# Attention of a macaron block on eight cores: q and k of four heads made with tokens on partitions and turned by DMA transposes

## The chip, the cores and the metric

One Trainium2 chip; the program runs on eight of its NeuronCores, one sequence of the batch on each, and the cores exchange nothing. The metric is the device time of the slowest core in microseconds. TensorE does the matmuls (PE in the profile), VectorE (DVE), ScalarE (ACT) and GpSimd (POOL) the rest, and SyncE (SP) issues DMAs. DMAs are issued from SP and from POOL; those of POOL also convert the f32 weights to bf16.

## The reference

The input x is 8 x 2048 x 1024. Three layers follow one another; this is the core of them:

```python
x = x + 0.5 * ffn(layernorm(x))          # r = sigmoid(xr W_r), k = relu(xk W_k)^2, r * (k W_v)
# attention, 16 heads, dh = 64, rank r = 48
x = layernorm(hidden, ln1_g, ln1_b)
Q = einsum('bsd,dhr,hre->bhse', x, q_U, q_V) + q_b
K = einsum('bhsr,hrd->bhsd', einsum('bsd,dhr->bhsr', x, k_U), k_V) + k_b
V = einsum('bhsr,hrd->bhsd', einsum('bsd,dhr->bhsr', x, v_U), v_V) + v_b
scores = einsum('bhse,bhte->bhst', Q, K) / 8, causal; attn = softmax(scores)
attn_out = ctx @ out_U @ out_V + out_b;  h = hidden + attn_out
h + (gelu(layernorm(h) @ fc1_U @ fc1_V + fc1_b) @ fc2_U @ fc2_V + fc2_b)
x = x + 0.5 * ffn(layernorm(x))          # the same weights again
```

## The kernel before

The kernel has four stages on each core: phase 0 (the first ffn), phase 1 (attention), phase 2 (output projection and MLP), phase 3 (the second ffn). Every engine runs a program of its own, in order; semaphores tie them together. Tokens are worked in four blocks of 512. The normalised input of attention lies in x1T, features on partitions, 8 chunks of 512 tokens for each block.

Scores are computed in the rank space: the q weight is Wq = q_U (q_V k_V^T), 49 wide with a column for the k bias, so that a head's score is the product of a 49-row q and a 49-row k. Two heads are a pair (p, 0 to 7); they lie at partitions 0 and 64. Before the change a unit Q or K makes q or k of one pair for one block: for each chunk c, two matmuls with 64 weight columns each and 512 tokens moving. It comes out with features on partitions, VectorE adds the bias on eviction from PSUM and writes Qr or Kr (two buffers of each), and scores read them there. A unit V makes v of eight heads for 128 tokens with tokens as weights and 384 columns of vU moving.

All this is laid out by a planner. Attention of a pair is 20 steps; a step g is two tiles of 128 keys by 512 queries of both heads. In a step TensorE does the scores of two tiles (pe_qk), then the pieces of other units that slots[g] lists, then the context of the step before (pe_av). ScalarE turns each tile into exponentials (act_exp), two PSUM tiles SD taking turns; VectorE multiplies the diagonal tiles by a mask, evicts units (dve_unit) in the order of their last matmul, and normalises. Within a pair, step 20p + j(j+1) + n belongs to query block j; its last two steps are on the diagonal and have fewer columns. fill() gives each step g a budget scale(g) * room(g), with room 4 for a full step, 3.5 and 2 for the diagonal ones; matmuls(u) and weight(u) are the chunks of a unit and the price of one; each job has a first step and a due step. Units use two PSUM banks UB in turn, so a unit starts when the unit before its neighbour is evicted (u_ev). The units early run in the last block of phase 0, prelude ahead of step 0. Other units: G and Wq build the q weight, A, ob, bo, W fold the output weights, fb folds a bias, after which VectorE scales f1U.

SP issues in phase 0 the transposes of x1T and the spills of X to DRAM (sp_tr, sp_spill), in phase 1 the packs of the normalised context into CN (sp_pack: four or five small copies for each pair and block). POOL issues the weight loads in an order written out by hand (pool_pair_weights, pool_phase1), tied to the count of scores (pool_at). In the last pair it reloads the spilled rows into S.

## Time and profile before

| what | value |
|---|---|
| median of 3 runs | 1071.65 us (1070.51 to 1195.31) |
| the profiled execution | 1070.4 us |
| its span, slowest of 8 cores | 1068.6 us (1064.0 to 1068.6) |
| TensorE busy in the span | 1016.2 us (95%) |
| VectorE, ScalarE, GpSimd busy | 549.5, 537.0, 187.5 us |
| granted clock of TensorE, eight cores | 0.992 to 0.995 |
| matmul instructions | 6278 |

The time is device time; the span goes from the first to the last instruction of one core, and the two differ by 1.8 us in the profiled execution. A granted clock of 1.0 is TensorE's upper level (2.4 GHz), 0.5 the lower (1.2 GHz). The busy time of an engine counts overlapping instructions once.

### The profile page before, as it was taken

To read this page: it belongs to the slowest core of one execution; us is meant where nothing else is said; L and a number is where in the kernel's file an instruction comes from. 1 tells how busy PE (TensorE), PEld (TensorE's weight loads), DVE (VectorE), ACT (ScalarE), POOL (GpSimd) and SP (SyncE) were. 2 spreads that over 40 slices of the span, in tenths; PEclk is the share of its full clock that TensorE was granted. 3 is DMA by queue.
4 is the path that set the end of the run, shared out by engine and by line. 5 is a ranking of instruction groups with operands and counts; after the bars stand their busy time and mean duration, and the time that the engine had idled before them with its cause. 6 is when DMAs were issued, how large, how long until landed. Compare 5 with 4: busy or idle time off the path is not lost.

```text
span 1068.6 us, 16930 instructions; the slowest of 8 cores (1064.0 to 1068.6 us)
## 1 busy us (share of the span) xinstructions
PE 1016.2 (95%) x6278; PEld 459.5 (43%) x6278; DVE 549.5 (51%) x1013; ACT 537.0 (50%) x646; POOL 187.5 (18%) x185
## 2 busy tenths in 40 slices
PE   3999999999999999898998999999999999999998
PEld 1444444454444444344343444444444444444443
DVE  6568979654646546566368980012120433734523
ACT  2335354267777787876775454333333354341321
POOL 2021423400000001110022137670000000023030
PEclk9999999999999999999999999999999999999999
DMA  9982377642110116750087899952300026041212
GB/s 167 209 220 69 90 142 164 121 100 69 31 27 17 28 28 98 110 81 9 8 207 213 112 123 154 211 96 48 63 16 1 1 40 115 5 119 79 40 79 79
DMA packets 94686, 95.89 MB, mean 90 GB/s; under 512 B 67856, under 2 KB 75152, under 8 KB 93328
## 3 DMA queue, kind: packets, MB, share of 16 engines
q0 software_dynamic: 20112, 52.74, 27.4%
q1 hardware_dynamic: 74496, 42.07, 17.0%
q8 instruction: 54, 0.88, 0.3%
q14 instruction: 24, 0.20, 0.1%
HBM read 91.94 MB, written 16.78 MB: 102 GB/s over the span
## 4 chain that ended last, share of the span: by engine, by line
PE 74%; DVE 14%; issue 5%; ACT 4%; DMA 2%; SPq 1%; DVEq 0%; ACTq 0%
PE ub L905 11%; PE db L1414 10%; PE db L1380 10%; PE db L355 7%; PE db L369 7%; PE sd L1040 7%; PE db L381 6%; PE ct L1075 5%; PE ub L915 3%; DVE st L420 3%; PE db L1393 3%; ACT AT L1050 2%; PE db L1367 2%; PE db L1352 2%; PE ub L957 2%
## 5 line engine op out<-in xcount | busy, mean ns | idle before, releaser
L1050 ACT ACTIVATE AT<-sd 128x1024 bf16<-128x1024 f32 (+1 forms) x320 | 267.7, 897 | 83.2 <-PE sd L1040 82.8
L1463 ACT ACTIVATE HM<-db,csts 128x512 bf16<-128x512 f32 x128 | 80.8, 683 | 138.9 <-PE db L1380 138.9
L1414 PE MATMUL db<-HM,f2U 128*128 128x512 bf16 x512 | 120.3, 379 | 1.3 <-ACT HM L1463 1.3
L1380 PE MATMUL db<-P,f1V 128*128 128x512 bf16 x512 | 120.3, 379 | 1.0 <-ACT P L1451 1.0
L1040 PE MATMUL sd<-Qr,Kr 64*128 64x512 bf16 (+3 forms) x640 | 96.1, 352 | 9.3 <-ACT AT L1050 8.6
L1075 PE MATMUL ct<-AT,VA 128*64 128x512 bf16 (+3 forms) x640 | 87.1, 351 | 3.5 <-DVE AT L1057 3.5
L1414 PEld LDWEIGHTS db<-HM,f2U 128*128 128x128 bf16 x512 | 49.9, 98 | 62.1 <-issue 2.9
L1380 PEld LDWEIGHTS db<-P,f1V 128*128 128x128 bf16 x512 | 50.0, 98 | 61.7 <-issue 1.7
L1557 DVE CAST P<-db 128x1024 bf16<-128x1024 f32 x4 | 4.9, 1224 | 137.9 <-PE db L1414 137.9
L905 PE MATMUL ub<-x1T,Wq 128*64 128x512 bf16 x512 | 69.3, 389 | 1.8 <-DVE tta L409 1.6
L905 PE MATMUL ub<-x1T,kU 128*64 128x512 bf16 x512 | 67.2, 383 | 0.1
L355 PE MATMUL db<-XKa,wk 128*128 128x512 bf16 x256 | 57.6, 387 | 5.6 <-DVE XKa L470 5.6
L414 POOL TENSOR_TENSOR X<-X,tta 128x1024 f32<-128x1024 f32 x16 | 43.5, 2736 | 105.9 <-DVE XKa L470 90.6
L1040 PEld LDWEIGHTS sd<-Qr,Kr 64*128 64x128 bf16 x640 | 28.5, 93 | 77.0 <-issue 71.6
L369 PE MATMUL db<-wr,XRa 128*128 128x512 bf16 x256 | 58.1, 387 | 0.6 <-DVE XRa L484 0.6
L381 PE MATMUL db<-wv,KAa 128*128 128x512 bf16 x256 | 56.0, 379 | 1.4 <-DMA wv<-wvT 1.4
L355 PE MATMUL db<-XKb,wk 128*128 128x512 bf16 x256 | 56.1, 379 | 0.0
L369 PE MATMUL db<-wr,XRb 128*128 128x512 bf16 x256 | 55.9, 379 | 0.0
L390 ACT ACTIVATE krla<-db 128x1024 bf16<-128x1024 f32 x16 | 16.4, 1023 | 74.4 <-PE db L355 52.4
L381 PE MATMUL db<-wv,KAb 128*128 128x512 bf16 x240 | 52.6, 379 | 0.1
L915 PE MATMUL ub<-vU,x1T 128*64 128x384 bf16 x512 | 48.5, 329 | 2.0 <-DVE VA L991 1.1
L1075 PEld LDWEIGHTS ct<-AT,VA 128*64 128x64 bf16 x640 | 35.4, 110 | 33.1 <-issue 8.6
(161 smaller groups left out, 1335.4 us busy)
## 6 DMA issues: line engine op xcount, KB each, us to landing
S<-xs POOLq DMA_DIRECT2D x32, 512.0 KB, 10.1
xs<-X SPq DMA_DIRECT2D x4, 2048.0 KB, 9.2
x_out<-S SPq DMA_DIRECT2D x15, 512.0 KB, 2.6
wr<-wrT POOLq DMA_DIRECT2D x4, 1024.0 KB, 18.8
X<-x_in SPq DMA_DIRECT2D x2, 2048.0 KB, 13.9
f1V<-fc1V POOLq DMA_DIRECT2D x16, 256.0 KB, 4.4
f2U<-fc2U POOLq DMA_DIRECT2D x32, 128.0 KB, 6.3
CN<-cs SPq DMA_DIRECT2D x112, 24.0 KB
```

Source lines behind the costliest of these rows:

```text
L355: m = pe.matmul(DB[p][:, TB * h:TB * (h + 1)], f.wk(c, dk), f.XK[:, TB * c:TB * (c + 1)], start=c == 0, stop=c == CH - 1)
L369: m = pe.matmul(DB[2 * t % 4][:, TB * h:TB * (h + 1)], XR[:, TB * c + 128 * t:TB * c + 128 * (t + 1)], f.wr(c)[:, TB * h:TB * (h + 1)], st ...
L381: m = pe.matmul(DB[2 * t % 4 + 1][:, TB * h:TB * (h + 1)], f.KA[:, TB * c + 128 * t:TB * c + 128 * (t + 1)], f.wv(c)[:, TB * h:TB * (h + 1 ...
L414: pool.tensor_tensor(xt, xt, f.tt[(4 * b + t) % len(f.tt)][:, :], ALU.add)._wait_ge(F.kv, 4 * b + t + 1).then_inc(F.add, 1)
L905: m = pe.matmul(bank[o:o + 64, :], w[:, 128 * c + o:128 * c + o + 64], x1T[j][:, TB * c:TB * (c + 1)], start=c == 0, stop=c == CH - 1)
L915: m = pe.matmul(bank[o:o + 64, 0:384], x1T[t // 4][:, x0:x0 + 64], vU[:, w0 + 384 * c:w0 + 384 * (c + 1)], start=c == 0, stop=c == CH - 1)
L1040: m = pe.matmul(SD[q % 2][:, TB * s + off:TB * (s + 1)], Kr[p % 2][64 * s:64 * s + 64, 128 * i:128 * (i + 1)], Qr[p % 2][64 * s:64 * s + 6 ...
L1050: act.activation(c3(AT[q % 4])[:, :, off:TB], c3(SD[q % 2])[:, :, off:TB], AF.Exp, scale=0.125)._wait_ge(a_qk, q + 1).then_inc(a_exp, 1)
L1075: m = pe.matmul(CT[k % 2][64 * s:64 * s + 64, off:TB], VA[p // 4][:, 512 * i + 64 * h:512 * i + 64 * (h + 1)], AT[q % 4][:, TB * s + off:T ...
L1380: m = pe.matmul(bank[:, TB * e:TB * (e + 1)], f1V[ic // 8][:, 1024 * pc + 128 * (ic % 8):1024 * pc + 128 * (ic % 8 + 1)], P1[b][:, TB * pc ...
L1414: m = pe.matmul(DB[2 + p2 // 2][:, TB * (p2 % 2):TB * (p2 % 2 + 1)], f2U[ic // 8][:, 512 * (ic % 8) + 128 * p2:512 * (ic % 8) + 128 * (p2 ...
L1463: m = act.activation(HM[i % 4][:, TB * e:TB * (e + 1)], DB[job_db[("H", b, i)]][:, TB * e:TB * (e + 1)], AF.Gelu_apprx_tanh, bias=scol("fc ...
```

## The change

Q and K units are replaced by QK units. A group G is four heads (pairs 2G and 2G+1). QK(G, t) makes q and k of the four heads for 128 tokens: the tokens of x1T are the weights (two halves of 64), and the 8 x 49 = 392 columns of WQK (GC) move, q and k weights of the pairs side by side. VectorE adds qbB, a row of biases repeated on all partitions, and writes the result into a quarter of ST, each 49 columns padded to 64; ST's padding is cleared once, at the end of phase 0. Then SP issues two DMA transposes of 128 x 256 (sp_qk), one for each pair, into one of three pair buffers QS (q in the first 2048 columns, k in the second). Scores of an even pair wait for the transposes (d_qt) at each query block; a VectorE eviction waits until the transposes four units earlier have landed. The weights of a group come by pool_group_weights: one load of WQK with zero columns in the q places, which the evictions of Wq then fill, and two of qUT. Four Wq and a qb are made for each group. The planner gets new prices, due steps and scales: 1.12 up to step 130 and 0.85 from 131 to 156; V of the upper heads may start at step 12, A at step 92, and W is spread over steps 131 to 156. Some buffers move to other places, and the loads of vVT, outV, fc1_V and the last group's weights take other points in POOL's order. sp_phase1 interleaves the transposes with the packs.

The core of the diff:

```diff
+GC = 8 * (RQ + 1)
...
-    kUp = np.zeros((128, NP, CH, 128), np.float32)
+    kUp = np.zeros((128, NP // 2, CH, 2, 2, 2, RQ + 1), np.float32)
     for h in range(NH):
         s, p = h % 2, h // 2
-        kUp[:, p, :, 64 * s:64 * s + RQ] = kU[:, h, :].reshape(CH, 128, RQ).transpose(1, 0, 2)
+        kUp[:, p // 2, :, p % 2, 1, s, :RQ] = kU[:, h, :].reshape(CH, 128, RQ).transpose(1, 0, 2)
...
-    Qr = [at("Qr%d" % i, T, BF16, 24 + 8 * i) for i in range(2)]
-    Kr = [at("Kr%d" % i, T, BF16, 28 + 8 * i) for i in range(2)]
+    QS = [at("QS%d" % i, 2 * T, BF16, (24, 32, 176)[i]) for i in range(3)]
     CN = [at("CN%d" % b, 6 * TB, BF16, (40, 48, 56, 160)[b]) for b in range(NB)]
     cs = [at("cs%d" % b, TB, BF16, (46, 54, 62, 166)[b]) for b in range(NB)]
     vU = at("vU", 2 * CH * 384, BF16, 72)
-    Wq = [at("Wq%d" % i, 1024, BF16, 84 + 2 * i) for i in range(2)]
+    ST = at("ST", 4 * 512, BF16, 84)
+    WQK = at("WQK", CH * GC, BF16, 120)
+    qbB = at("qbB", GC, F32, 126.125)
     VA = [at("VA%d" % i, NT * 512, BF16, 88 + 16 * i) for i in range(2)]
-    qUT = [at("qUT%d" % i, D, BF16, 120 + 2 * i) for i in range(2)]
-    kU = [at("kU%d" % i, 1024, BF16, 124 + 2 * i) for i in range(2)]
+    qUT = [at("qUT%d" % i, D, BF16, (142, 140)[i]) for i in range(2)]
     qVT, kVTb = at("qVT", 1024, BF16, 136), at("kVTb", 1024, BF16, 138)
-    Gs, vVT = at("Gs", 1024, BF16, 140), at("vVT", 1024, BF16, 142)
+    qbr = at("qbr", 1024, BF16, 136)
+    Gs, vVT = at("Gs", 1024, BF16, 128), at("vVT", 1024, BF16, 130)
...
+        for t in range(4):
+            sp_qk(sp, 0, t)
...
+        dve.memset(ST[:, :], 0.0).then_inc(q_z, 1)
+        dve.memset(qbB[:, :], 0.0).then_inc(q_z, 1)
+        dve.memset(qbB[:, :].rearrange("p (i k s e) -> p i k s e", i=2, k=2, s=2)[:, :, 1, :, RQ:RQ + 1],
+                   1.0)._wait_ge(q_z, 2).then_inc(q_z, 1)
...
+            if i == 1:
+                dve.wait_ge(d_bconst, 16)
+                dve.tensor_copy(qbr[:, :].rearrange("p (q e) -> p q e", e=128),
+                                bsl("qb", 0, NP).unsqueeze(2).to_broadcast([128, NP, 128])).then_inc(q_z, 1)
...
-    early = [("G", 0), ("G", 1), ("qb",), ("Wq", 0, 0), ("Wq", 0, 1)]
-    prelude = [("Q", 0, 0), ("K", 0, 0)] + [("V", 0, t) for t in range(4)]
+    early = [("G", 0), ("G", 1), ("Wq", 0, 0), ("Wq", 0, 1), ("Wq", 1, 0), ("Wq", 1, 1), ("qb", 0)]
+    prelude = [("QK", 0, t) for t in range(4)] + [("V", 0, t) for t in range(4)]
...
-        return [("Q", 0, j), ("K", 0, j)] + [("V", 0, t) for t in range(4 * j, 4 * j + 4)]
+        return [(kind, 0, t) for kind in ("QK", "V") for t in range(4 * j, 4 * j + 4)]
     def matmuls(u):
-        return {"Q": CH, "K": CH, "V": CH, "W": 6}.get(u[0], 1)
+        return {"QK": CH, "V": CH, "W": 6}.get(u[0], 1)
...
-        return {"V": 0.75, "Wq": 1.5, "A": 1.5, "ob": 6, "bo": 6, "fb": 12}.get(u[0], 1)
+        return {"QK": 0.77, "V": 0.75, "Wq": 1.0, "qb": 0.5, "A": 1.5, "ob": 6, "bo": 6, "fb": 12}.get(u[0], 1)
...
-    def pair_jobs(p):
-        due = [step_of(p, j, 0) - 2 for j in range(NB)]
-        jobs = [(STEPS * (p - 1) - 2, STEPS * (p - 1) + 1 if p > 1 else due[0], ("Wq", p, h))
-                for h in range(2)]
-        for kind in "QK":
-            jobs += [(STEPS * (p - 1), due[j], (kind, p, j)) for j in range(NB)]
+    def group_jobs(G):
+        g = STEPS * (2 * G - 1)
+        jobs = [(g - 4, g + 1, ("Wq", p, h)) for p in (2 * G, 2 * G + 1) for h in range(2)]
+        jobs += [(g - 4, g + 1, ("qb", G))]
+        jobs += [(g, step_of(2 * G, t // 4, 0) - 3, ("QK", G, t)) for t in range(NT)]
         return jobs
-    fill([(0, 1, u) for u in block_units(1)], 0, 1, lambda g: 8.0)
-    fill([(2, 5, u) for u in block_units(2)], 2, 5, lambda g: 3.2)
-    fill([(6, 11, u) for u in block_units(3)], 6, 11, lambda g: 2.1)
-    jobs = [j for p in range(1, NP) for j in pair_jobs(p)]
-    jobs += [(STEPS, step_of(4, t // 4, 0) - 2, ("V", 1, t)) for t in range(NT)]
-    merge = [("A", jc, h) for jc in range(6) for h in range(2)] + [("ob",), ("bo", 0), ("bo", 1), ("fb",)]
-    jobs += [(STEPS * 5 + 4, STEPS * 7 - 1, u) for i, u in enumerate(merge)]
-    fill(jobs, 11, STEPS * 7 - 1, lambda g: 1.5 if g < 88 else 1.35)
-    fill([(STEPS * 7, STEPS * 7 + 13, ("W", hc, h)) for hc in range(6) for h in range(2)],
-         STEPS * 7, STEPS * 7 + 13, lambda g: 1.6)
+    fill([(0, 1, u) for u in block_units(1)], 0, 1, lambda g: 9.0)
+    fill([(2, 5, u) for u in block_units(2)], 2, 5, lambda g: 3.7)
+    fill([(6, 11, u) for u in block_units(3)], 6, 11, lambda g: 2.35)
+    jobs = [j for G in range(1, NP // 2) for j in group_jobs(G)]
+    jobs += [(12, step_of(4, t // 4, 0) - 2, ("V", 1, t)) for t in range(NT)]
+    merge = [("A", jc, h) for jc in range(6) for h in range(2)] + [("ob",)]
+    jobs += [(STEPS * 4 + 12, STEPS * 6 - 1, u) for u in merge]
+    jobs += [(STEPS * 6 + 4, STEPS * 7 - 1, u) for u in (("bo", 0), ("bo", 1), ("fb",))]
+    jobs += [(STEPS * 6 + 11, STEPS * 8 - 4, ("W", hc, h)) for hc in range(6) for h in range(2)]
+    fill(jobs, 12, STEPS * NP - 4, lambda g: 1.12 if g < STEPS * 6 + 11 else 0.85)
...
-        elif kind in ("Q", "K"):
-            p, j = u[1], u[2]
-            if p == 0 and i0 == 0:
-                pe.wait_ge(b_aff, j + 1)
-            if kind == "K":
-                if j == 0 and i0 == 0:
-                    pe.wait_ge(d_ku[p % 2], 16 * (p // 2 + 1))
-                w = kU[p % 2]
-            else:
-                if j == 0 and i0 == 0:
-                    pe.wait_ge(u_ev, done("Wq", p, 1))
-                w = Wq[p % 2]
+        elif kind == "QK":
+            G, t = u[1], u[2]
+            if i0 == 0:
+                if t == 0:
+                    pe.wait_ge(u_ev, done("Wq", 2 * G + 1, 1))
+                if G == 0 and t % 4 == 0:
+                    pe.wait_ge(b_aff, t // 4 + 1)
             for c in range(i0, i1):
                 for o in (0, 64):
-                    m = pe.matmul(bank[o:o + 64, :], w[:, 128 * c + o:128 * c + o + 64],
-                                  x1T[j][:, TB * c:TB * (c + 1)], start=c == 0, stop=c == CH - 1)
+                    x0 = TB * c + 128 * (t % 4) + o
+                    m = pe.matmul(bank[o:o + 64, 0:GC], x1T[t // 4][:, x0:x0 + 64],
+                                  WQK[:, GC * c:GC * (c + 1)], start=c == 0, stop=c == CH - 1)
...
+            if u[1] == 0:
+                pe.wait_ge(q_z, 4)
+            for i in range(2):
+                p = 2 * u[1] + i
+                m = pe.matmul(bank[:, 128 * i:128 * (i + 1)], qbr[:, 128 * p:128 * (p + 1)],
+                              kVTb[:, 128 * p:128 * (p + 1)], start=True, stop=True)
         elif kind == "Wq":
             p = u[1]
...
-            m = dve.tensor_copy(qbias[:, :], bank[:, 0:NP])
+            if u[1] == 0:
+                dve.wait_ge(q_z, 3)
+            m = dve.tensor_copy(
+                qbB[:, :].rearrange("p (i k s e) -> p i k s e", i=2, k=2, s=2)[:, :, 0, :, :],
+                bank[:, 0:256].rearrange("p (i s e) -> p i s e", i=2, s=2)[:, :, :, 0:RQ + 1])
...
+            p, h = u[1], u[2]
+            if p % 2 == 0 and h == 0:
+                dve.wait_ge(d_ku, 16 * (p // 2 + 1))
+            dst = WQK[:, GC * 4 * h:GC * 4 * (h + 1)].rearrange("p (c e) -> p c e", e=GC)
+            o = 4 * (RQ + 1) * (p % 2)
+            m = dve.tensor_copy(
+                dst[:, :, o:o + 2 * (RQ + 1)].rearrange("p c (s e) -> p c s e", s=2),
+                bank[:, :].rearrange("p (c s e) -> p c s e", c=4, s=2)[:, :, :, 0:RQ + 1])
+        elif kind == "QK":
+            G, t = u[1], u[2]
+            n = NT * G + t
+            if t == 0:
+                dve.wait_ge(u_ev, done("qb", G))
+            if n >= 4:
+                dve.wait_ge(d_qt[t % 4], 32 * (n // 4))
+            else:
+                dve.wait_ge(q_z, 3)
+            dst = ST[:, 512 * (t % 4):512 * (t % 4 + 1)].rearrange("p (h e) -> p h e", e=64)
+            m = dve.tensor_tensor(dst[:, :, 0:RQ + 1],
+                                  bank[:, 0:GC].rearrange("p (h e) -> p h e", e=RQ + 1),
+                                  qbB[:, :].rearrange("p (h e) -> p h e", e=RQ + 1), ALU.add)
...
-            pe.wait_ge(u_ev, max(done("Q", p, j), done("K", p, j)))
+        if i == 0 and p % 2 == 0:
+            for k in range(4):
...
+                pe.wait_ge(d_qt[k], 32 * (2 * p + j + 1))
...
+                          QS[p % 3][64 * s:64 * s + 64, T + 128 * i:T + 128 * (i + 1)],
+                          QS[p % 3][64 * s:64 * s + 64, TB * j + off:TB * (j + 1)],
...
+    def sp_qk(sp, G, t):
+        if t == 0 and G == 0:
+            for b in (1, 2):
+                sp.wait_ge(d_sp[b], 16)
+                sp.wait_ge(F0.z, 4 * group("B", b) + 4)
+        if t == 0 and G == 1:
+            sp.wait_ge(F0.add, 16)
+        if t == 0 and G:
+            sp.wait_ge(a_qk, 40 * (2 * G - 1))
+        sp.wait_ge(u_ev, done("QK", G, t))
+        for i in range(2):
+            sp.dma_start_transpose(c3(QS[(2 * G + i) % 3], T)[:, :, 128 * t:128 * (t + 1)],
+                                   ST[:, 512 * (t % 4) + 256 * i:512 * (t % 4) + 256 * (i + 1)]).then_inc(
+                                       d_qt[t % 4], 16)
     def sp_phase1(sp):
+        for p, j, n in steps():
+            g = step_of(p, j, n)
+            for u, i0, i1 in slots[g]:
+                if u[0] == "QK" and i1 == matmuls(u):
+                    sp_qk(sp, u[1], u[2])
+            for k in range(32):
+                if last_step[k] + NORM == g:
+                    sp_pack(sp, k)
         for k in range(32):
-            sp_pack(sp, k)
+            if last_step[k] + NORM >= STEPS * NP:
...
+    def pool_group_weights(pool, G):
+        if G:
+            pool.wait_ge(u_pe, done("QK", G - 1, NT - 1))
+        pool.dma_start(WQK[:, :], dram["kU"][:, CH * GC * G:CH * GC * (G + 1)]).then_inc(d_ku, 16)
+        for p in (2 * G, 2 * G + 1):
+            pool.dma_start(qUT[p % 2][:, :], dram["qUT"][:, D * p:D * (p + 1)]).then_inc(d_qu[p % 2], 16)
...
+                    pool_group_weights(pool, 0)
...
+        pool_group_weights(pool, 1)
+        pool.dma_start(bo_bc[:, :], dram["outb_row"].partition_broadcast(128)).then_inc(d_bc, 16)
+        pool.dma_start(fb_bc[:, :], dram["fc2b_row"].partition_broadcast(128)).then_inc(d_bc, 16)
+        pool_group_weights(pool, 2)
...
+            if jc == 3:
+                pool_group_weights(pool, 3)
...
+        for q in (1, 0):
             for i in range(4):
-                pool_at(pool, 5, 8 + 3 * (4 * q + i))
+                pool_at(pool, 6 - q, 8 + 6 * i)
...
+            pool.wait_ge(u_pe, max(done("QK", 3, NT - 1), done("ob")))
+            for k in range(4):
+                pool.wait_ge(d_qt[k], 32 * NT)
```

## Rows read from the trace of the kernel before

**Rows 1.** Windows, attention: length, busy (count) of five engines, clock, DMA share, GB/s.
```profile
216.00:574.00 358.00, 340.33 (x3104) 152.79 (x3100) 198.96 (x409) 274.55 (x326) 31.05 (x59) 0.99 0.34 68
```

**Rows 2.** Windows, pairs 1, 4 and 5, first exponential to first exponential.
```profile
273.87:317.68 43.81, 42.99 (x384) 18.92 (x382) 23.42 (x47) 33.65 (x40) 2.13 (x4) 1.00 0.20 34
...
404.09:443.81 39.72, 36.79 (x310) 15.31 (x308) 20.30 (x43) 33.23 (x40) 9.52 (x18) 1.00 0.81 118
443.81:489.06 45.25, 41.54 (x406) 18.96 (x404) 27.67 (x56) 33.61 (x40) 4.24 (x8) 1.00 0.44 67
```

**Rows 3.** Timeline of PE, two steps of pair 1: start, us, engine, line.
```profile
305.50 0.61 PE L1040 MATMUL sd<-Qr,Kr 64*128 64x512 bf16 x4
306.04 1.49 PE L905 MATMUL ub<-x1T,kU 128*64 128x512 bf16 x12
307.36 0.60 PE L1075 MATMUL ct<-AT,VA 128*64 128x512 bf16 x4
307.89 0.60 PE L1040 MATMUL sd<-Qr,Kr 64*128 64x512 bf16 x4
...
308.88 1.14 PE L915 MATMUL ub<-vU,x1T 128*64 128x384 bf16 x12
```

**Rows 4.** Timeline of PE, steps with no unit, at the end of pair 4.
```profile
436.88 0.39 PE L1040 MATMUL sd<-Qr,Kr 64*128 64x512 bf16 x2 [0.52 <-ACT AT L1050]
...
438.71 0.39 PE L1040 MATMUL sd<-Qr,Kr 64*128 64x512 bf16 x2 [0.52 <-ACT AT L1050]
```

**Rows 5.** Timeline of PE, prelude and step 0.
```profile
213.09 2.79 PE L915 MATMUL ub<-vU,x1T 128*64 128x384 bf16 x32 [0.51 <-DVE VA L991]
215.81 0.55 PE L1040 MATMUL sd<-Qr,Kr 64*128 64x512 bf16 x4
216.29 1.92 PE L905 MATMUL ub<-x1T,Wq 128*64 128x512 bf16 x16
```

**Rows 6.** Groups by line, PE: busy, mean ns of one, idle before.
```profile
L905 PE MATMUL ub<-x1T,kU 128*64 128x512 bf16 x512 | 67.2, 383 | 0.1
```

**Rows 7.** Timeline of PE, a lightly filled step of pair 4.
```profile
430.39 0.79 PE L1040 MATMUL sd<-Qr,Kr 64*128 64x512 bf16 x4
...
432.53 0.77 PE L1040 MATMUL sd<-Qr,Kr 64*128 64x512 bf16 x4
```

**Rows 8.** Timeline of PE around A and Wq units, pair 5.
```profile
474.35 0.85 PE L924 MATMUL ub<-vVT,oU 128*128 128x128 bf16 x8 [0.64 <-DVE AoT L995]
...
485.58 0.62 PE L950 MATMUL ub<-oV,oB 128*64 128x512 bf16 x4 [0.86 <-DVE Wq L970]
```

**Rows 9.** Windows, after fb.
```profile
503.00:510.00 7.00, 6.30 (x32) 2.09 (x32) 2.96 (x7) 4.57 (x5) 0.00 (x0) 0.52 0.05 12
```

**Rows 10.** Timeline of PE, last block of phase 0.
```profile
180.94 0.34 PE L879 MATMUL ub<-bcst,kVTb 128*128 128x1 bf16 x8 [1.34 <-DVE Gs L966]
```

**Rows 11.** Timeline of DVE, last block of phase 0.
```profile
181.20 2.66 DVE L550 TENSOR_SCALAR x1T<-x1T,csts 128x512 bf16<-128x512 bf16 x8
...
183.86 0.68 DVE L970 CAST Wq<-ub 128x512 bf16<-128x512 f32 x1
...
190.64 2.70 DVE L550 TENSOR_SCALAR x1T<-x1T,csts 128x512 bf16<-128x512 bf16 x8 [2.47 <-DMA x1T<-zt]
```

**Rows 12.** DMA issues, 208 to 222: KB each, us to landing.
```profile
xs<-X SPq DMA_DIRECT2D x1, 2048.0 KB, 11.0
...
x1T<-zt SPq DMA_TRANSPOSE x4, 4.8
```

**Rows 13.** DMA issues, 182 to 190.
```profile
x1T<-zt SPq DMA_TRANSPOSE x4, 3.2
```

**Rows 14.** DMA issues, 420 to 440.
```profile
kU<-kU POOLq DMA_DIRECT2D x1, 256.0 KB, 8.4
```

**Rows 15.** Timeline of SP, four transposes in a row, phase 3.
```profile
949.20 5.39 SPq L1580 DMA_TRANSPOSE zTb<-zu  x4
```

**Rows 16.** DMA issues, 147 to 170.
```profile
x1T<-zt SPq DMA_TRANSPOSE x4, 13.9
```

82 lines of the change are left out of this document (23 added, 59 removed).

## The prediction, made before the kernel ran

> **What bounds it now.** The cores lie within 0.4% of each other, so one core tells of all. First I read the window of the whole attention stage [rows 1]: TensorE is busy 340.3 of its 358 us, ScalarE 274.6, VectorE 199.0. TensorE's order of work is the path there, and only its busy time or its gaps can give time back. The stage behind (574 on) keeps its code and I leave it as it is. Second, the stretches of single head pairs, each with 40 exponentials [rows 2]: pair 1 takes 43.8 us with TensorE full, pair 4 takes 39.7 with a gap of 2.9, pair 5 takes 45.3 with a gap of 3.7. ScalarE needs some 33.5 us of each. Third, single steps in the timeline, because a step is what the planner fills. A full step with six chunk pairs of projection lasts 2.39 us, scores to scores, and TensorE never waits in it [rows 3]. A full step with no projection lasts 1.83 us, with a wait of 0.52 for the exponential [rows 4]. So filled steps are TensorE's and empty ones ScalarE's.
>
> **Price of a chunk.** A chunk pair is the two half-column matmuls of one chunk. Old Q or K: 8 pairs take 1.92 us [rows 5], 6 take 1.49 [rows 3], so 0.215 each. V is built as the new units are (tokens as weights, 384 columns moving): 16 pairs take 2.79 us [rows 5], 6 take 1.14 [rows 3], so 0.165. The new unit moves 392 columns: 0.168. The number of pairs stays: 256 for K, which is the 512 matmuls of its row [rows 6], and as many for Q; new, 4 groups x 16 x 8 = 512. Saved on TensorE: 512 x 0.047 = 24 us.
>
> **How steps turn that into time.** A full step holds scores (0.53), the fill F, context (0.53) [rows 3]. Between the empty and the crowded step neither engine is full: scores of one step wait for exponentials of the step before, and behind them on TensorE lie fill and context. I take the largest of 1.83, 1.64 + F/2 and 1.07 + F; the middle one is half of two exponentials (1.94) plus TensorE's chain (1.34 + F). The step at 430.39 has F 0.87 and measured 2.14 [rows 7]; the formula gives 2.07. Diagonal steps go alike with floors of 1.73 and 0.87. The planner is arithmetic in the code, so I worked both plans out from it. The old one has F about 1.3 in most full steps and leaves 17 steps empty; the new one has 1.0 in most, 0.65 to 0.87 in the last 25, and leaves 12 empty. By pair the old steps sum to 56.1, 42.9, 42.8, 42.9, 39.1, 41.1, 40.4, 40.0 = 345; measured 358, and the 13 between are lumps, below. The new ones: 59.2, 38.5, 38.8, 38.6, 37.0, 38.6, 38.8, 35.6 = 325. So the steps give 20 us: the 24 of TensorE and 5 of gaps, less 9 that full steps near 2.1 lose in the chain between two engines.
>
> **Lumps.** A unit's bank must be evicted before the next but one unit starts. Old: A units, three or four to a step, wait 0.64 for VectorE's eviction, two Wq 0.86 [rows 8]. The new plan puts four Wq and one qb into steps 16, 56 and 96: three evictions on the path, some 1.8 us a time, 5.4 in all against 3 for the old ones. A units: 2.0 against 3. After fb came f1U's scaling in front of a mask and half the clock for 7 us [rows 9]: 3 us; the scaling now meets no diagonal step: 1.5. First steps and last context stay at 3.3. New 12, old 12.5: nothing.
>
> **End of phase 0.** VectorE gets two clears ahead of G's evictions, for which TensorE already waits 1.34 us [rows 10]. The trace has no clear of this size. ST is 2048 bf16 columns; x1T's scaling does 512 in 0.33 (2.66 for 8) and Wq's cast in 0.68 [rows 11], so 1.4 to 2.7; I take 2.0, as a clear has no bf16 source to profit from, and 0.4 for qbB. On the path 2.4, bounds 1.5 and 3.2. The Trainium skill, page "VectorE: DVE Perf Modes", section "Zero memsets can be issued as uint32 (trn2)", says that a clear takes a cycle per element whatever the type; by it the clear is nearer the upper bound, and the sum half a microsecond longer. Two more Wq and a larger qb: 0.6 on TensorE. qbr's copy and three evictions (some 2.7 us) are hidden by VectorE's wait of 2.47 for x1T [rows 11] and its waits for phase 0's matmuls; without that cover 2 us. Sum +3.
>
> **Start of attention.** The prelude is 32 x (0.168 + 0.165) against 16 x 0.215 + 32 x 0.165: +1.9. Then the first scores wait for eight transposes. SP issues block 3's 2 MB spill just before them; it landed 11.0 us after issue, and the x1T transposes behind it 4.8 after theirs [rows 12], against 3.2 on a quiet queue [rows 13]. Spill at 211, landed by 221, transposes 1 us behind; V covers TensorE until 219.9. Stall 2.0, bounds 0 and 6. The old wait of 0.51 for V's eviction goes [rows 5]. First scores 215.8 + 3 + 1.9 + 2.0 - 0.5 = 222.2, +6.4.
>
> **Elsewhere.** Each later group's first use comes at least seven steps (15 us) behind its last eviction, against 3 to 8 us of landing: nothing; without that cover some 3 us at each of 12 gates. On SP, the packs (4 or 5 issues each) now stand between the transposes, in step order. VectorE's new wait for a quarter of ST has masks and normalisations behind it, and TensorE's context waits for those; four units are 12 us. WQK and qUT of the last group go out at step 91 among outV and f1U, where a 256 KB load took 8.4 us [rows 14]; they are needed at step 96, 11 us on: 0.5. S8's reload waits for the last W, now 7 us before the end of attention instead of 13; the next stage has 21 us before it: nothing, or 2 if it delays x2T.
>
> **Sum.** 1068.6 - 20 + 6.4 + 0.5 = 1055.5 of span. The profiled run took 1.8 more than its span, so 1057.3, and the median is 1.25 above that run: 1058 (-1.3%). Within 2% is about what a measurement of this kernel can't tell from no change.
>
> **Rivals.** (a) The forecast, 1058, with 1051 to 1065: 0.50.
> (b) All is covered: clears at the lower bound, no stall at the start, the Wq steps as cheap as the formula: 1058 - 1 - 2 - 5.4 - 1.5 (fb) = 1048. For it: VectorE is busy little over half of attention. Against: such steps cost in the old trace. 0.18.
> (c) A small transpose costs SP what a large one does: four took 5.39 us to issue [rows 15], 1.35 each. Eight end at 222.3 and land by 225, +3; four of x1T and eight more hold step 2 until 241 instead of 237, +5: 1066. Against: the small ones hold a quarter of the data. The Trainium skill, "DMA: Bandwidth & Descriptors", section "Rules for kernel authors", says that transfers under 64 KB pay mostly overhead and are best joined; these are 64 KB. 0.15.
> (d) The steps don't give it back: freed matmul time becomes waits for exponentials, full steps at 2.2 instead of 2.1. 90 x 0.1: 1067. Against: [rows 7]. 0.10.
> (e) Slower: the ring of four. Behind a spill and loads four transposes took 13.9 us to land [rows 16]. Once landing and eviction exceed four units' pitch, 12.8 us, VectorE stops and its masks with it. At 17.6 a unit costs 4.4 us instead of 3.2: 48 x 1.2 = 58, about 1115. Against: a pair's DMA share of 0.20 [rows 2]. 0.07.
>
> Faster by over 2% (under 1050): (b) and the edge of (a), 0.19. Slower: (e), 0.07. Same: 0.74. The range 1044 to 1072 leaves out (e) and the far ends of (b), (c) and (d).
>
> **What would show it.** QK runs of 16 matmuls in 1.5 us; full steps 2.1 apart; first scores near 222, behind a wait for a DMA; steps 16, 56, 96 over 3.5; G's eviction 2.4 later. It is wrong if TensorE waits for transposes after step 0, or VectorE for ST, or if the clears cost nothing.

## The result: slower by 5.3%, and the profile after

| what | value |
|---|---|
| median of the changed kernel | 1129.01 us (4 runs), before beside it 1071.79 us |
| ratio | 1.0533, 95% interval 1.0509 to 1.0557 |
| predicted | 1058 us, range 1044 to 1072 |
| profiled execution | 1127.43 us, span of its slowest core 1125.8 us |
| spans of the cores | 1115.3 to 1125.8 us, granted clock 0.965 to 0.974 |

In some executions, of the kernel before and of changed ones alike, the cores of one die ran at a lower granted clock and some per cent longer; the ratios leave these out, and so do the times of experiments 3 and 6, where they would move the median by 4 and 7 us.

The kernel is slower, and on all cores. The first view is the window of the attention stage and of what follows it, on core 3: length, then busy time (count) of PE, PEld, DVE, ACT and POOL, the granted clock, the DMA share and GB/s.

```profile
216.00:630.00 414.00, 337.49 (x3122) 160.39 (x3118) 185.43 (x408) 273.51 (x327) 28.14 (x54) 0.93 0.40 77
630.00:1125.00 495.00, 486.81 (x2244) 219.26 (x2244) 189.81 (x315) 177.76 (x237) 104.08 (x91) 1.00 0.41 83
```

Attention grew from 358 us [rows 1] to some 403 (first scores 228.08, last context 630.9; before 215.8 and 573.6), and the stages behind it are as long as they were. TensorE is busy no longer than before, 337.5 against 340.3 us, and that at a granted clock of 0.93 against 0.99, so it has indeed less to do. It stands still for 76 us of the window, where it stood for 18. What it waits for is the next view, the waits of PE and DVE in attention (total us, times, longest):

```profile
PE sd L1066 <- DMA QS<-ST: 43.4, 7, 14.0
PE sd L1066 <- ACT AT L1076: 16.3, 46, 0.5
PE ct L1101 <- DVE AT L1083: 9.3, 7, 3.1
...
DVE ST L1009 <- DMA QS<-ST: 40.3, 15, 4.7
```

Scores (sd) wait seven times for the transposes of q and k. VectorE waits fifteen times for a quarter of ST that a transpose still has to read; behind these waits stand masks, and TensorE waits for masks in its turn (the third row; before, 3.5 us in four waits). These are two of the signs that the prediction gave for being wrong. The chain that ended last, by engine and by line, names a queue:

```profile
PE 50%; SPq 18%; DVE 14%; DMA 8%; issue 6%; ACT 3%; POOL 1%; DVEq 0%; ACTq 0%; POOLq 0%
SPq L1166 12%; PE db L1471 10%; PE db L1437 9%; PE db L384 5%; PE db L358 5%; SPq L1148 5%; PE db L372 4%; DMA X<-x_in 4%; DMA QS<-ST 3%; PE sd L1066 3%; DVE st L423 3%; PE db L1450 2%; PE ct L1101 2%; PE ub L931 2%; PE db L1424 2%
```

L1166 issues the transposes of q and k, L1148 the packs. SP's timeline in pair 1 and the first part of pair 2 shows how (start, length, line, count):

```profile
317.63 4.96 SPq L1166 DMA_TRANSPOSE QS<-ST  x4
322.69 3.65 SPq L1148 DMA_DIRECT2D CN<-cs  x5
326.44 5.56 SPq L1166 DMA_TRANSPOSE QS<-ST  x4
332.10 3.62 SPq L1148 DMA_DIRECT2D CN<-cs  x5
335.82 10.38 SPq L1166 DMA_TRANSPOSE QS<-ST  x8
346.29 3.62 SPq L1148 DMA_DIRECT2D CN<-cs  x5
350.01 14.03 SPq L1166 DMA_TRANSPOSE QS<-ST  x10
```

There is no gap between the rows: the queue is full from 317 to 384 us. A transpose of 128x256 takes 1.2 us to issue, a pack 0.72, so a QK unit (two transposes) and its share of packs cost SP 4.2 us (the 16 units of group 1 in 67 us), where the plan brings a unit every 3.2 us. A second kind of loss is at the ends of the groups, here step 92, the first scores that read the last transposes of group 2, in PE's timeline, and SP's and POOL's issues before it:

```profile
468.35 0.57 PE L1101 MATMUL ct<-AT,VA 128*64 128x512 bf16 x4
482.91 1.04 PE L1066 MATMUL sd<-QS 64*128 64x512 bf16 x4 [13.99 <-DMA QS<-ST]
```
```profile
467.51 3.53 SPq L1166 DMA_TRANSPOSE QS<-ST  x2
```
```profile
467.51 0.53 POOL L1241 DMA_DIRECT2D WQK<-kU  x1 [1.31 <-PE sd L1066]
```

The last two transposes go out in the same instant as the 784 KB weight load of the next group and land 12 to 14 us later; the median of all is 2.4. The same happens at steps 12 (wait 10.55 us) and 52 (4.86). The weight load is not alone there: two 256 KB loads of qUT go with it, at step 92 five loads of outV (256 KB each) too, and at step 12 two broadcast loads of biases (512 KB each). After a long wait the matmuls run at 1.2 GHz for a while: the granted clock is 0.50 from 484 to 490 us.

The sums by pair, in us from first scores to first scores (the last one to the last context); "formula" are the steps as the prediction worked them out:

| pair | 0 | 1 | 2 | 3 | 4 | 5 | 6 | 7 |
|---|---|---|---|---|---|---|---|---|
| before | 57.6 | 43.8 | 43.5 | 43.0 | 39.7 | 45.3 | 43.8 | 41.1 |
| formula | 59.2 | 38.5 | 38.8 | 38.6 | 37.0 | 38.6 | 38.8 | 35.6 |
| changed | 80.9 | 41.0 | 51.8 | 40.6 | 62.7 | 40.9 | 47.1 | 37.9 |

Pairs 1, 3, 5 and 7, which begin with buffers filled long ago, have become shorter than before, as meant, though 2.0 to 2.5 us longer than the formula. Pairs 0, 2, 4 and 6, where a new group begins, carry the loss.

### The profile page after: what moved, and what is told of

It reads as the page before. It is cut to its first block, busy times and chain, and to the rows that moved or that the text cites. A ratio compares the mean times of both kernels' runs of the same rounds, so it can differ in the third digit from the quotient of the medians.

```text
span 1125.8 us, 17161 instructions; the slowest of 8 cores (1115.3 to 1125.8 us)
## 1 busy us (share of the span) xinstructions
PE 1007.9 (90%) x6217; PEld 466.7 (41%) x6278; DVE 540.7 (48%) x1020; ACT 536.0 (48%) x646; POOL 185.8 (17%) x181
## 3 DMA queue, kind: packets, MB, share of 16 engines
q0 software_dynamic: 19536, 53.85, 26.4%
## 4 chain that ended last, share of the span: by engine, by line
PE 49%; SPq 21%; DVE 15%; issue 7%; DMA 5%; ACT 3%; POOL 0%; DVEq 0%; ACTq 0%
SPq L1166 13%; PE db L1471 9%; PE db L1437 9%; PE db L358 6%; SPq L1148 6%; PE db L384 5%; PE db L372 5%; DMA QS<-ST 3%; DVE st L423 3%; PE db L1450 2%; PE sd L1066 2%; PE db L1424 2%; PE ub L931 2%; SPq L602 2%; PE ct L1101 2%
## 5 line engine op out<-in xcount | busy, mean ns | idle before, releaser
L1066 PE MATMUL sd<-QS 64*128 64x512 bf16 (+3 forms) x640 | 105.4, 368 | 62.7 <-DMA QS<-ST 44.7
L921 PE MATMUL ub<-WQK,x1T 128*64 128x392 bf16 x1024 | 107.1, 347 | 2.1 <-DVE tta L412 1.6
L1066 PEld LDWEIGHTS sd<-QS 64*128 64x128 bf16 x640 | 29.9, 94 | 137.6 <-issue 132.9
L1009 DVE TENSOR_TENSOR ST<-ub,qbB 128x392 bf16<-128x392 f32 x64 | 36.1, 566 | 94.0 <-PE ub L921 47.8
L1437 PEld LDWEIGHTS db<-P,f1V 128*128 128x128 bf16 x512 | 50.0, 98 | 61.7 <-issue 1.7
L921 PEld LDWEIGHTS ub<-WQK,x1T 128*64 128x64 bf16 x1024 | 54.3, 114 | 47.3 <-issue 25.8
L417 POOL TENSOR_TENSOR X<-X,tta 128x1024 f32<-128x1024 f32 x16 | 43.5, 2735 | 107.3 <-DVE XKa L473 88.9
L931 PE MATMUL ub<-vU,x1T 128*64 128x384 bf16 x512 | 51.3, 343 | 1.2 <-DVE VA L1016 0.8
## 6 DMA issues: line engine op xcount, KB each, us to landing
X<-x_in SPq DMA_DIRECT2D x2, 2048.0 KB, 12.7
```

The lines of the kernel that those rows point to most:

```text
L921: m = pe.matmul(bank[o:o + 64, 0:GC], x1T[t // 4][:, x0:x0 + 64], WQK[:, GC * c:GC * (c + 1)], start=c == 0, stop=c == CH - 1)
L931: m = pe.matmul(bank[o:o + 64, 0:384], x1T[t // 4][:, x0:x0 + 64], vU[:, w0 + 384 * c:w0 + 384 * (c + 1)], start=c == 0, stop=c == CH - 1)
L1066: m = pe.matmul(SD[q % 2][:, TB * s + off:TB * (s + 1)], QS[p % 3][64 * s:64 * s + 64, T + 128 * i:T + 128 * (i + 1)], QS[p % 3][64 * s:64 ...
L1437: m = pe.matmul(bank[:, TB * e:TB * (e + 1)], f1V[ic // 8][:, 1024 * pc + 128 * (ic % 8):1024 * pc + 128 * (ic % 8 + 1)], P1[b][:, TB * pc ...
```

## The experiments

Theory A: SP pays for each transpose whatever its size; transposes and packs fill its queue, and all that is late follows from that. Theory B: the next group's weight loads, and the loads that GpSimd sends beside them, sent when the last QK matmul is done, meet the last transposes in the DMA engines. Theory C, the rival to both: the lighter steps themselves don't give time back, or lose the clock. Times are medians; the kernel before was timed beside each (1070.9 to 1071.9 us).

**1. Price by size.** The kernel before, with 32 more transposes of zt into an unused tile, in fours of 1024, 512, 256 and 128 columns, two rounds of them:

```diff
+for n, w in enumerate((1024, 512, 256, 128)):
+    for i in range(4):
+        sp.dma_start_transpose(DM[:, 1024*i:1024*i + w].rearrange(...), zt[i][:, 0:w]).then_inc(d_dm, 16)
+    sp.wait_ge(d_dm, 64 * (n + 1) + 256 * (k - 7))
```

> The kernel before, with 32 more DMA transposes on SP in pairs 1 and 2 (twice: four of 128 x 1024, four of 128 x 512, four of 128 x 256, four of 128 x 128, each four waited for), from zt into unused space. Theory A (SP pays a price for each transpose whatever its size): all sizes take 1.15 to 1.3 us to issue, and land in 2.2 to 3.2 us. Rival (issue goes with the data): 1.25, 0.6, 0.3 and 0.2 us. The time stays within 1% of before by both, as nothing waits for these.

Measured: 1085.44 us (one execution). The second round, SP's group of these lines in four windows, from 1024 columns down to 128 (ns min/median/max to issue, and below us to landing):

```profile
L1133 SPq DMA_TRANSPOSE DM<-zt x4: 1280/1332/2147, 361.5 to 365.5; - x4
DMA to landing us min/median/max: 3.2/4.1/4.7
...
L1133 SPq DMA_TRANSPOSE DM<-zt x4: 1191/1269/1272, 369.6 to 373.5; - x4
DMA to landing us min/median/max: 2.5/2.5/3.1
...
L1133 SPq DMA_TRANSPOSE DM<-zt x4: 1170/1246/2336, 376.0 to 380.9; - x4
DMA to landing us min/median/max: 2.4/2.9/3.7
...
L1133 SPq DMA_TRANSPOSE DM<-zt x4: 1121/1234/1234, 383.4 to 387.1; - x4
DMA to landing us min/median/max: 2.2/2.4/2.4
```

An eighth of the data costs SP 0.1 us less. That is theory A's price, shown. The kernel's time missed what was expected of it (within 1%; it is 1.3% over), and VectorE's timeline shows the same kind of wait: a normalisation stood 18 us for packs that were queued behind the added transposes, and TensorE 14.3 us for an eviction behind it.

```profile
394.44 0.69 DVE L1099 TENSOR_TENSOR cs<-ct,rb 128x512 bf16<-128x512 f32 x1 [18.21 <-DMA CN<-cs]
```

**2. Weights later.** The changed kernel, one edit:

```diff
 pool.wait_ge(u_pe, done("QK", G - 1, NT - 1))
+for k in range(4):
+    pool.wait_ge(d_qt[k], 128 * G)
 pool.dma_start(WQK[:, :], ...)
```

> The changed kernel; the load of the next group's WQK and qUT now waits until the last transposes of the group before have landed. Theory B (the long waits at steps 12 and 92 are landings of 9 to 14 us beside that load): the landings fall to 2.3 to 4 us and the time falls by 15 to 25 us, to 1104 to 1114. Theory A alone (SP's queue is what is late): the last transposes are issued just as late, and the time falls by less than 5 us.

Measured: 1114.59 us, 1.041 of before (1.0385 to 1.0434): 14 us back, just short of the 15 to 25 expected of theory B and far over the 5 of theory A alone. On core 6, the slowest, the transposes issued from 268 to 281 us land like this, where in the changed kernel those of step 12 took up to 12.3 us:

```profile
L1166 SPq DMA_TRANSPOSE QS<-ST x8: 1169/1219/1255, 268.3 to 280.6; - x8
...
DMA to landing us min/median/max: 2.3/2.3/2.4
```

The waits are read from core 0, because core 6 had a granted clock of only 0.81 from 250 to 354 us, and a slower TensorE hides a part of them. There the wait at step 12 fell from 10.55 to 2.2 us, that at step 52 from 4.9 to 3.4 and that at step 92 from 14.0 to 4.2. Theory B holds, for a part. It doesn't single out the weights: all that stands behind them in GpSimd's order, the biases and outV, goes out later too. What it leaves is A's: VectorE still waits 45.4 us for ST, in sixteen places.

```profile
DVE ST L1009 <- DMA QS<-ST: 45.4, 16, 5.5
```

**3. Packs off SP.** The changed kernel with sp_pack called in POOL's program; pack_to issues the packs that are due by a step:

```diff
-for k in range(32):
-    if last_step[k] + NORM == g:
-        sp_pack(sp, k)
 def pool_at(pool, p, i):
+    pack_to(pool, STEPS * p + i // 2 - 1)
     pool.wait_ge(a_qk, 40 * p + i)
```

> The changed kernel with the 144 small copies of the packs issued from POOL, at the same steps, instead of SP. Theory A (transposes and packs together, some 1.2 and 0.75 us of issue each, fill SP wherever QK units are made): waits of the scores at steps 41, 51, 81, 121 and 131 go, those beside the WQK load shrink by what SP was behind, 15 to 30 us less, 1099 to 1114. Theory B alone: within 5 us of 1129.

Measured: 1095.35 us (1091.99 to 1104.17), 1.0247 (1.0171 to 1.0324): by the ratios some 31 us back, uncertain by 8. VectorE no longer waits for ST at all, and TensorE's waits for masks are down from 9.3 to 1.4 us; TensorE's waits for transposes are 26.4 us, and their longest, 11.1, is B's at step 12:

```profile
PE sd L1066 <- DMA QS<-ST: 26.4, 6, 11.1
PE sd L1066 <- ACT AT L1076: 17.1, 50, 0.5
```

The transposes are as many and as large as in the changed kernel. It is the queue that they shared: SP's timeline of the same stretch now has thirty transposes in 46.8 us, 3.1 us for a unit.

```profile
316.03 46.84 SPq L1166 DMA_TRANSPOSE QS<-ST  x30
```

A part of B's loss went with it. The wait at step 92 is 3.7 us instead of 14.0, because the last transposes of group 2 go out at 446.5 us, 7 us ahead of the weight load, which waits for step 91 (453.5 us). In the changed kernel the late queue had carried them into that load. At step 12 the load comes when the last QK matmul is done, and the collision stayed.

**4. Fewer transposes.** The changed kernel with one transpose of 128x512 per unit in group 0, one of 128x256 in group 1 and none in groups 2 and 3. It leaves part of the work out: scores of the later heads are computed from old q and k.

```diff
+if G == 0:
+    sp.dma_start_transpose(c3(QA, T)[:, :, 128 * t:128 * (t + 1)],
+                           ST[:, 512 * (t % 4):512 * (t % 4 + 1)]).then_inc(d_qt[t % 4], 16)
-for i in range(2):
+for i in range(1 if G == 1 else 0):
```

> The changed kernel with one transpose of 128 x 512 for each unit of group 0, one of 128 x 256 for group 1 and none for groups 2 and 3, so scores of the later heads are computed from stale q and k; all matmuls, evictions, packs and loads stay. Theories A and B together (the loss is all in the transposes): attention comes back to the steps' own 325 plus lumps of 12 to 15 us, and the time is 1055 to 1070. Rival C (lighter steps themselves lose, through half the clock and waits for exponentials): it stays above 1085.

Measured: 1082.20 us, 1.0091 (1.0062 to 1.0121): 12 us above the range expected of theories A and B together, and below the 1085 of theory C. PE's waits name most of it: 8.6 us of step 12 stayed, B's collision in group 0, and 2.8 at the first scores.

```profile
PE sd L1071 <- ACT AT L1081: 16.8, 49, 0.5
PE sd L1071 <- DMA QA<-ST: 11.4, 2, 8.6
```

Pair 4 takes 46.6 us against the formula's 37.0, though no transpose is issued in it. Most of this is in steps 92 to 97, with the A and Wq units: TensorE waits there for evictions, 0.5 to 1.4 us each, and in step 96 for two loads of qUT (2.2 us). That part of the loss is not the transposes'.

**5. Half the issues for the same bytes.** In groups 0 and 3 the two buffers become neighbours, and one transpose serves both:

```diff
+QA = at("QA", 4 * T, BF16, 24)
+QS = [QA[:, 0:2 * T], QA[:, 2 * T:4 * T], at("QS2", 2 * T, BF16, 176)]
...
+if G in (0, 3):
+    sp.dma_start_transpose(c3(QA, T)[:, :, 128 * t:128 * (t + 1)],
+                           ST[:, 512 * (t % 4):512 * (t % 4 + 1)]).then_inc(d_qt[t % 4], 16)
+    return
```

> The changed kernel, with the two buffers of groups 0 and 3 made neighbours, so that each QK unit of these groups is turned by one DMA transpose of 128x512 instead of two of 128x256; the bytes are the same. By the theory that SyncE pays 1.2 us for a transpose whatever its size, groups 0 and 3 put 32 transposes fewer (38 us of SyncE) in the queue: the first scores come some 3 us earlier (the last of four landings instead of eight), the waits in steps 121 and 131/132 go, about 8 us, and groups 1 and 2 stay as they are, with step 41 at +4 and step 81 at +3. The wait of 10 us at step 12 and that of 14 at step 92 stay, since the group's weight loads cause them: 1112 to 1120 us. If it were the bytes of the transposes or their time in the DMA engines that made them late, nothing would change: 1129.

Measured: 1109.56 us, 1.0357 (1.0339 to 1.0376): 19.5 us back, more than the 9 to 17 expected. The first scores come at 223.8 instead of 228.1, the waits in steps 121 and 131/132 are gone, and steps 41 and 81 still lose 2.4 to 3 us (over experiment 8's), much as expected. Not foreseen: the wait at step 12 fell by 2.3 us too, and that at step 92 by 1.6. The bytes are the same, so it isn't bytes that were late. The Trainium skill, "DMA: Bandwidth & Descriptors", section "Rules for kernel authors", says that many small transfers are best joined, since under 64 KB one pays mostly overhead; the trace agrees that joining pays, and it paid at 64 KB and over: what SP's queue pays is 1.2 to 1.3 us from 32 KB to 256 KB (experiment 1).

**6. The edits of experiments 2 and 3 together**, in the changed kernel:

```diff
+for k in range(4):
+    pool.wait_ge(d_qt[k], 128 * G)
...
+    pack_to(pool, STEPS * p + i // 2 - 1)
```

> The changed kernel with the two edits made alone before put together: the packs are issued from GpSimd, and the next group's weights are loaded after the group's last transposes have landed. If the SyncE queue and the collision with the weight loads are two causes that add up, it comes to 1129 - 29 - 14 = 1086 us, perhaps 5 more because both edits shorten the wait at step 92; the pairs then take about 69, 40, 42, 40, 41, 40, 40 and 38 us, and a wait of 7 us for the first scores is left. If one of them is only another face of the other, it comes out near the better one alone, 1100 us.

Measured: 1080.44 us (1080.17 and 1080.71), 1.0084 (1.0062 to 1.0105): 48 us back, where 31 + 14 = 45 would be the sum, within the 8 us by which experiment 3 is uncertain. In total the two add up, but not place by place. At step 92 they are two ways to the same 10 us (3.7, 4.2, and 4.5 with both); pair 4, which holds it, took 62.7 us, 47.8 with the packs moved, 52.9 with the loads late (core 0), and takes 47.7 with both. In pair 0 they do add up: 80.9, 79.4, 71.9 and 70.1. PE's waits for transposes are down to three, of 13.6 us in all, 6.8 of them the start.

**7. The spill behind the first transposes**, in the changed kernel:

```diff
-sp_spill(sp, NB - 1)
 for t in range(4):
     sp_qk(sp, 0, t)
+sp_spill(sp, NB - 1)
 sp_tr(sp, "B", NB - 1)
```

> The changed kernel with one edit: SyncE issues the spill of the last block behind the transposes of the first four QK units, not ahead of them. If the spill's 7.7 us in the DMA engines hold the first transposes up, the first scores come 3 to 5 us earlier (224 us in the trace, a wait of 3 to 4 us instead of 7.5), and the kernel ends 3 to 5 us earlier, 1124 to 1126. If it is SyncE's eight issues at 1.2 us each behind the last eviction of a QK unit that set the first scores, they move by under 1 us: 1128 to 1129.

Measured: 1131.21 us, 1.0554 (1.0534 to 1.0574): 3 to 5 us were expected, nothing came. PE's timeline shows both halves: the first wait fell from 7.55 to 2.72, as expected, and the next one, at step 2, rose from 2.85 to 9.07.

```profile
225.43 0.55 PE L1066 MATMUL sd<-QS 64*128 64x512 bf16 x4 [2.72 <-DMA QS<-ST]
...
248.14 1.04 PE L1066 MATMUL sd<-QS 64*128 64x512 bf16 x4 [9.07 <-DMA QS<-ST]
```

The transposes of units 4 to 7 stand behind the spill and the four of x1T, and start at 235.4 instead of 232.5. The wait was moved down the queue.

**8. All so far**: the diffs of experiments 2, 3, 5 and 7 in one kernel, with the wait of experiment 2 for the smaller count:

```diff
-    pool.wait_ge(d_qt[k], 128 * G)
+    pool.wait_ge(d_qt[k], qt(4 * G))
```

> The changed kernel with everything so far: packs issued from GpSimd, group weights loaded after the last transposes have landed, one transpose for each unit in groups 0 and 3, and the spill of the last block put behind the first four units' transposes. Against the two edits alone it gains the start: the first scores at 221 to 224 us instead of 228. Groups 0 and 3 then have no late transpose at all. By the theories together 1074 to 1084 us, still not below the kernel before (1071.7), because the lightly filled steps run at half clock in places and the four Wq units in one step cost 1.5 us three times. If the clock comes back too, it falls to 1060.

Measured: 1074.52 us, 1.0029 (1.0019 to 1.004), at the good end of the 1074 to 1084 expected. Left: 4.5 us at step 2 (experiment 7's), 2.9 at step 92, where the outU and outV loads run.

**9. The start in another order**, in the changed kernel alone. The last block's spill goes tile by tile from 200.7 us, and x1T's last four transposes behind those of units 4 to 7:

```diff
-sp_spill(sp, NB - 1)
+for k in range(4):
+    sp.wait_ge(F0.add, 12 + k + 1)
+    sp.dma_start(xs[128*(12+k):128*(13+k), :], X[:, D*(12+k):D*(13+k)]).then_inc(d_sp[3], 16)
 for t in range(4):
     sp_qk(sp, 0, t)
-sp_tr(sp, "B", NB - 1)
...
 sp_qk(sp, u[1], u[2])
+if g == 1: sp_tr(sp, "B", NB - 1)
```

> The changed kernel with the start's edit alone (the last block's spill by tiles as they are added, and its four x1T transposes behind the transposes of QK units 4 to 7). If the late first transposes come from the spill and the order of SyncE's queue, the first scores come at 223 to 225 us instead of 228, and the steps 0 to 2, 6.7 us over their matmuls now, lose 4 us of that: 1119 to 1122 us. If the time is only moved, as when the whole spill went behind them, it stays at 1128 to 1131 with the wait at step 2 instead.

Measured: 1125.65 us, 1.0515 (1.0498 to 1.0533): 3.4 us back of the 7 to 10 expected. First scores at 224.2 and the wait at step 2 down to 2.15 are as expected; but step 12 of the profiled run waited 11.6 instead of 10.6, and step 92 15.1 instead of 14.0. The waits at the groups' ends come from the same full queue and the same loads, and seem to have taken back part of what was won before them; no run separates this. In experiment 10, without them, pair 0 is 7.0 us shorter than in experiment 8, with first scores 1.8 us later (profiled on other cores).

**10. Start and loads, on top of experiment 8.** The start of experiment 9; group 3's weights first, the outU loads behind them, outV from step 92, f1U from step 100, A units from step 98 (the plan's last scale 1.02 instead of 0.85 to fit):

```diff
 pool.wait_ge(a_av, 160)
+pool_group_weights(pool, 3)
 for i in range(6):
-    pool_at(pool, 4, 4 + 2 * i)
     pool.dma_start(oU[:, 1024 * i:1024 * (i + 1)], ...)
...
-    pool_at(pool, 4, 16 + 2 * jc)
-    if jc == 3:
-        pool_group_weights(pool, 3)
+    pool_at(pool, 4, 24 + 2 * jc)
...
-jobs += [(STEPS * 4 + 12, STEPS * 6 - 1, u) for u in merge]
+jobs += [(STEPS * 4 + 18, STEPS * 6 - 1, u) for u in merge]
```

> The version with everything so far (packs from GpSimd, weights late, one transpose per unit in groups 0 and 3; 1074.5 us), with two more edits. At the start, the spill of the last block goes tile by tile as each is added, ahead of the first transposes, and the last block's four x1T transposes go behind those of QK units 4 to 7. Around step 92, the weights of group 3 are loaded first, the outU loads behind them instead of beside group 2's last transposes, and the A units from step 98 on. If landings late by collision and by place in the SyncE queue are all that is left of the waits, the 4.5 us at step 2 with the half clock after it (7 us) and the 2.9 us at step 92 with the slow steps 93 and 94 (7 us) go: 1058 to 1064 us, below the kernel before (1071). If the time goes elsewhere for another reason (the lightly filled steps themselves losing the clock), it stays at 1070 to 1075.

Measured: 1070.98 us, 1.0000 (0.9991 to 1.001): short of 1058 to 1064. The start did what was asked: pair 0 is 61.7 us, 2.5 over the formula. A part of the rest I lost myself, as PE's timeline at step 98 says: the outU loads, sent at 421.6 together with 1.3 MB of weights, took 13 to 20 us, and A units stood for them; the step took 7.25 us, where steps with three A units take 2.3 to 3.5 in experiment 12. Pairs 5 to 7, which this plan fills more, are 4.6 us longer than in experiment 8.

```profile
440.77 0.34 PE L1073 MATMUL sd<-QA 64*128 64x384 bf16 x2 [0.52 <-ACT AT L1083]
444.27 1.01 PE L947 MATMUL ub<-vVT,oU 128*128 128x128 bf16 x8 [3.16 <-DMA oU<-outU]
```

**11. Two Wq units in a step**, on top of that:

```diff
-"Wq": 1.0,
+"Wq": 2.2,
```

> The same, and the plan's weight of a Wq unit 2.2 instead of 1.0, so that it puts two of them into a step and not four and a qb. The three steps with four Wq units take 1.4 to 1.6 us more than their matmuls, because the units' evictions of 0.56 us follow one another through two banks; two in a step should hide: 3 to 4 us less than the kernel without this edit. If these steps lose their time to anything but the number of units in a step, no difference.

Measured: 1070.03 us against 1070.98, ratios 0.9989 (0.9979 to 0.9999) and 1.0000 to before: 1 us, and the intervals touch. In the traces steps 16 and 56 no longer exceed the formula (1.4 us each before), while step 98 waited longer, so what was won went there. As a total it's inconclusive.

**12. The outU loads early.** On top of experiment 11, with its order around step 92 changed back in part: all six outU loads at step 80, weights of group 3 and outV behind group 2's last transposes, the A units and the scales of the changed kernel again. Against the changed kernel:

```diff
 pool.wait_ge(a_av, 160)
 for i in range(6):
-    pool_at(pool, 4, 4 + 2 * i)
     pool.dma_start(oU[:, 1024 * i:1024 * (i + 1)], ...)
...
+pool_group_weights(pool, 3)
 for jc in range(6):
-    pool_at(pool, 4, 16 + 2 * jc)
-    if jc == 3:
-        pool_group_weights(pool, 3)
+    pool_at(pool, 4, 24 + 2 * jc)
```

> The version with two Wq units in a step, its order around step 92 changed back in part: the six outU loads go all at step 80, eight steps ahead of group 2's last transposes, the weights of group 3 and the outV loads come behind those transposes, and the A units and the rest of the plan are as in the changed kernel. In the version with outU loads late, step 98 waited 5.5 to 8.6 us for them (TensorE stood at the first A unit) and the squeezed plan cost about 5 us more in pairs 5 to 7. If that is what it lost, pairs 4 to 7 take about 41, 40, 40.6 and 38 us, the attention about 341 us instead of 352.6 and the kernel 1058 to 1062 us, some 1% below the kernel before. If the lightly filled steps lose the clock as soon as the waits are gone, it stays at 1068 to 1071.

Measured: 1061.18 us (1058.58 to 1065.92, 6 runs), 0.9905 of before (0.9883 to 0.9928). This is 1% faster than the kernel before. On its slowest core, 5, TensorE waits for no q or k in the whole stage; the window of it and the first waits of PE:

```profile
216.00:566.00 350.00, 323.48 (x3135) 156.84 (x3136) 188.76 (x414) 274.66 (x327) 100.56 (x195) 0.99 0.48 88
```
```profile
PE sd L1073 <- ACT AT L1083: 17.1, 52, 0.5
PE ub L947 <- DVE AoT L1027: 3.0, 4, 1.4
PE ct L1108 <- DVE AT L1090: 2.0, 4, 1.0
```

The pairs are 60.6, 39.8, 39.5, 39.8, 45.0, 40.5, 40.9 and 37.9 us, 344.0 in all; before 357.8, changed 402.8. The granted clock is 0.99 again with the same light steps, and on core 1 it is at the upper level from the first scores to the last context: theory C, that they lose the clock by themselves, falls. What is left of it is the 0.7 to 2.3 us by which the pairs exceed the formula, and 8.0 in pair 4. Nine transposes beside the outU loads still landed 6.1 to 12.7 us after issue, but no score of that core needed them so soon.

The two windows also say what a wait costs. From the changed kernel's 414 us to these 350 there are 50 us less of standing TensorE, and 14 us less of busy TensorE for the same matmuls (337.5 against 323.5). Those 14 go with the lower clock: in the changed kernel it was at 0.50 for 61 us of the stage, in eight stretches that begin in or just behind the long steps (0, 2, 11, 41, 51, 81, 91 and 131).

## Why the prediction was wrong

**The step that failed** is "Elsewhere", and in it one word, "nothing", for the first use of each later group. It compared the seven steps between a unit's eviction and its use with a landing of 3 to 8 us, and left out the queue between the two. The numbers for that queue stood in the prediction: 1.35 us for a transpose from [rows 15] in rival (c), "four or five issues each" for the packs. I did not multiply them. Over the whole stage 128 x 1.2 + 144 x 0.72 = 257 us of SP in 403 would still seem to leave room; but in a QK stretch a unit comes every 3.2 us and costs SP 4.2. With the packs gone from SP, some 31 us came back (experiment 3); with half the issues in two groups, 19.5 (experiment 5). The comparison of seven steps with the landing was itself sound: in experiment 12, with the packs gone from the queue, even transposes that took 12.7 us to land were in time on the slowest core. The sentence on VectorE ("four units are 12 us") left out the same queue: VectorE stood 40.3 us for ST.

**Rival (c)** had the price right (1.2 us at 256 columns, 1.25 at 1024) and its reach far too small: it followed the price through the start only, +8. **Rival (e)** had the mechanism, VectorE stopped before a quarter of ST with its masks behind it, and 1115 us; it gave landing in the DMA engines as the cause, and it had 0.07. The cause is the issue: landing is 2.4 us in the median. So its 1115 is near the measured 1129 without bearing out the reason it gave. The two were one case, and its chance should not have been split.

**WQK's loads** were priced at 0.5 us, for the wait of Wq for them. The changed kernel shows no such wait, since TensorE stood for transposes first; experiment 6 has 2.6 us of it and experiment 12 has 1.8. But what the loads do to others was asked only the other way round, load behind small transfers: the victims are the last transposes of the group, and keeping them apart gave 14 us (experiment 2).

**Start**: stall 7.55 us, against 2.0 with bounds 0 and 6. The spill was issued at 211.4 as said and landed at 219.1, before the 221 assumed; but those issued beside it took 4.0 to 8.9 us to land, and the eighth was issued at 225.5 only and landed at 227.8, eight issues being 9.6 us of SP. Rival (c)'s landing by 225 was the nearer one. The first four of the eight took 2.4 us each to issue in the median, beside the spill, where 1.2 is the rule. Experiment 7 shows the spill's part, some 5 us, and that the queue behind takes it back.

**What was right.** The chunk price: 64 matmuls of 392 columns take 5.50 us, 0.172 for two, against 0.168 said; their group averages 345 ns where Q and K had 383 [rows 6]. In experiment 12, with the stalls gone, TensorE is busy 16.9 us less than in [rows 1], though that window has 5.3 us of prelude in it which the other lacks: 22 of the 24 said. G's eviction: the two clears took 1.76 + 0.39 = 2.15 us, said 2.4, and the first QK unit starts 2.9 us later than its place before, said 3.

```profile
179.76 1.76 DVE L749 MEMSET ST<- 128x2048 bf16 x1 [0.38 <-issue]
181.56 0.39 DVE L750 MEMSET qbB<- 128x392 f32 x1
```

1656 elements more cost 1.38 us more, bf16 against f32, that is 0.83 ns for each; a third clear, of 4 f32 columns, took 0.06 us, and from it to the 392 columns it is 0.83 ns again. That is a price by element and not by byte, as the Trainium skill has it ("VectorE: DVE Perf Modes", section "Zero memsets can be issued as uint32 (trn2)"). The prediction made of that rule a sum half a microsecond longer; measured, the two clears were 0.25 us shorter than said.

Neighbouring full steps with 12, 10 and 12 of the new matmuls are 2.09, 2.14 and 2.25 us apart; the formula has 2.15, 2.07 and 2.15:

```profile
429.63 0.61 PE L1066 MATMUL sd<-QS 64*128 64x512 bf16 x4
430.17 1.19 PE L921 MATMUL ub<-WQK,x1T 128*64 128x392 bf16 x12
...
431.72 0.82 PE L1066 MATMUL sd<-QS 64*128 64x512 bf16 x4
432.47 1.02 PE L921 MATMUL ub<-WQK,x1T 128*64 128x392 bf16 x10
...
433.86 0.77 PE L1066 MATMUL sd<-QS 64*128 64x512 bf16 x4
434.56 1.19 PE L921 MATMUL ub<-WQK,x1T 128*64 128x392 bf16 x12
...
436.11 0.66 PE L1066 MATMUL sd<-QS 64*128 64x512 bf16 x4
```

Over the 59 full steps of pairs 1 to 7 that hold q, k or v work or none, the average is 2.20 in the changed kernel and 2.14 in experiment 12, where the formula has 2.10 and 2.11: without the queue, rival (d) had 0.03 us of its 0.1. The lumps of Wq were 1.4 to 1.6 each (said 1.8). So most terms of the sum hold. Experiment 12, which has the steps but no queue, comes to 1061 against the 1058 forecast, but this nearness is in part luck: that kernel has no stall at the start (said 2.0) and its Wq units spread out (two lumps of 1.8 fewer), so the same sum would give some 1052 for it, an estimate from the prediction's own terms. Against the forecast's 337.8 us, attention there is 344.0 on the slowest core, 4.6 of the 6.2 in steps 93 to 96, and 341.2 on core 1.

**Still open.** Whether the weight loads hold up the transposes beside them by their bytes, by their conversion or by their queue, no run separates; nor the weights from the loads behind them in GpSimd's order. Pair 4 exceeds the formula by 5.7 us on most cores in experiment 12 and by 8 on the slowest; A units' evictions of 0.5 to 1.4 us each are in it, the rest isn't resolved. How much of the 31 us of experiment 3 is transposes sooner and how much masks sooner can't be told apart by these runs.

## What to carry to other kernels

A queue that only issues DMAs is an engine with a busy time: before work is moved into it, add up its issues per unit of work (number times the measured time of one, not bytes) over the stretch where they come, with all that already stands in it, and compare with the unit's pitch, not with the average. A transfer that somebody soon waits for must not share its moment with a large load that nobody waits for yet; let the load wait for the landing. And where a change has a right core and a wrong neighbourhood, the profile that shows the loss can show the edits that bring the change out: here six of them together (packs to another queue, loads held back, joined transposes, the start's order, Wq units spread, outU early) took it from 1129 to 1061 us.

## What the runs showed of the hardware

- A DMA transpose from SBUF to SBUF cost its queue 1.12 to 1.34 us for 128, 256, 512 or 1024 columns in most cases (single ones up to 3.0), and mostly landed 2.2 to 2.4 us after issue at the small end, 3.2 and more at the large one (experiment 1). Four in a row are 5 us of SP.
- A copy of 8 to 24 KB cost SP 0.56 to 0.77 us in most cases, 0.72 in the median (changed kernel).
- 64 KB transposes issued within a few us of a 784 KB weight load, two of 256 KB and the loads behind them landed after 9.4 to 13.7 us instead of 2.4 (steps 12 and 92 of the changed kernel), and after 5.7 to 8.7 where no loads stood behind (step 52); beside a spill of 2 MB after 4.0 to 8.9.
- After TensorE had stood for 14 us the granted clock was 0.50 for the steps behind, to 492 us (eight matmuls of an A unit pair took 1.03 us there, 0.62 in experiment 12).
